# Two dense attentions of 16 heads, one head to 32 rows of the array, units prepared before the attention

## The chip, the core and the metric

The kernel runs on one core of one Trainium2 chip, as one launch. The metric is the device time of that launch in microseconds (us); lower is better. Engines are named as the profile names them: PE is the matrix engine and PEld its weight loads, DVE the vector engine, ACT the scalar engine, POOL GpSimd, SP the queue that issues DMAs.

## The reference, cut to what matters

Twelve sublayers transform x, four batches ("units") of 512 tokens by 128 channels, all in float32. The change is about two of them, the two dense attentions. Both have 16 heads of 8 channels. The first (`mqa`) is causal and shares one key and one value head among all 16; the second (`rope`) is not causal, has its own keys and values for each head, biases, and a rotation of queries and keys.

```python
latent = x @ Wc_down                       # mqa: 128 -> 64
q = (latent @ Wq_up).reshape(B, T, 16, 8); k, v = split(latent @ Wkv_up)
att = softmax(where(causal, einsum('bthd,bsd->bhts', q, k) / sqrt(8), -inf))
x = x + einsum('bhts,bsd->bthd', att, v).reshape(B, T, 128) @ Wc_proj

q, k, v = x @ Wq.T + bq, x @ Wk.T + bk, x @ Wv.T + bv      # rope, 16 heads of 8
att = softmax(einsum('bhsd,bhtd->bhst', rot(q) / sqrt(8), rot(k)))
x = x + einsum('bhst,bhtd->bhsd', att, v).reshape(B, S, 128) @ Wo.T + bo
```

Each input is first normalised over the 128 channels. The other ten sublayers (two mixtures of experts, two channel mixes, two gated MLPs, a forgetting attention, a time mix and two deep six-layer stacks, "deep") are not changed.

## The kernel before

Channels lie on the 128 partitions and tokens along the free dimension, so a unit is a tile of 128 x 512. All sublayers but deep run unit by unit in a hardware loop (`per_unit`), and each unit ends with a wait for its own x, so nothing of unit b + 1 overlaps unit b. Each engine has its own written order of instructions; semaphores tie them together. Every f32 product is issued to PE as two passes (two LDWEIGHTS, two MATMULs), which is why counts of f32 matmuls are twice the number of products.

In the dense attentions (`dense_pe`, `dense_act`, `dense_dve`, lines 410 to 582) a unit goes through these steps, each for all 16 heads:

1. Normalisation (`ln_pe`, `ln_act`, `ln_dve`, lines 141 to 197) and the products for queries, keys and values (lines 414 to 428). For each head DVE writes a copy of the keys in which all other rows are zero (line 556), so that a head's scores are a product over all 128 rows of the array.
2. **Scores for the maxima**: for each of 4 query tiles and 16 heads a product of 128 queries by up to 512 keys (line 444), four heads to four PSUM banks, of which DVE takes the row maxima (line 564). In `mqa` a bf16 product with the identity adds the causal mask to the diagonal block (line 447).
3. The negated maxima are turned by PE (line 452) and copied by ACT into free rows of the queries (line 500), so that the next scores come out with the maximum subtracted.
4. **Keys and values**: for each of 4 key tiles and 16 heads a product keys by queries (line 463, mask line 466), its exponential by ACT (line 506, four buffers), and the product of values with it (line 473), two steps behind. The values lie spread in zeroed columns (lines 511 to 517), so that this too uses the whole array; ones beside them give the denominators.
5. Copy, reciprocal, product (lines 569 to 574), the output projection (line 477) and the addition to x (lines 578, 580).

SP issues all DMAs: x, some 50 constant tensors (line 1297), then layers 0 and 1 of deep (line 1272). PE starts when all constants have landed.

## Time and profile before

| | us |
|---|---|
| median of 3 runs | 6653.96 |
| lowest and highest run | 6646.73, 6661.31 |
| profiled execution, its own time | 6652.98 |
| its span, first to last instruction | 6651.2 |
| of it, `mqa` with its four units | 644.0 (162.0 to 806.0) |
| of it, `rope` with its four units | 830.4 (1011.0 to 1841.4) |
| deep, twice | nearly all after 2300 |
| share of PE, DVE, ACT, POOL busy | 81%, 57%, 35%, 45% |
| granted PE clock, mean | 0.873 of 2.4 GHz |

The profiled execution's own time is 1.8 us more than its span; both are within the three runs. Busy shares are averages over very different stages; the stages have to be read one by one. A granted clock of 1.00 is 2.4 GHz and 0.50 is 1.2 GHz; means between them are mixtures of the two.

### The profile page before, as it was taken

Reading aid. Unit: us, or ns where it says so; the run is one execution under the profiler, and the core shown is the slowest. Engines: PE = TensorE matmul, PEld = TensorE weight load, DVE = VectorE, ACT = ScalarE, POOL = GpSimd, SP = SyncE. Lnnn points to the kernel's source line nnn. Section 1 sums busy time; section 2 is a strip of 40 time slices with the busy share of each in tenths; the row PEclk is TensorE's granted clock in tenths of the full one; section 3 lists DMA queues with packets and bytes.
Section 4 is the critical chain, followed back from the end, with each engine's and each line's share of the span. In section 5 each row is a group of like instructions: output and inputs, shape, how many; then the busy total and the mean of one; then the engine's idle time right before and its main releaser. Section 6 shows DMA issues by size and latency. Waiting matters only on the chain.

```text
span 6651.2 us, 145048 instructions
## 1 busy us (share of the span) xinstructions
PE 5355.9 (81%) x64980; PEld 3035.4 (46%) x64980; DVE 3759.9 (57%) x4061; ACT 2357.0 (35%) x2740; POOL 2981.6 (45%) x1264
## 2 busy tenths in 40 slices
PE   5888868898964678888888888856888888888887
PEld 2455533343432344554555545423455555545454
DVE  4222343321224377777777777645777777777774
ACT  1222221122232344444444444423444444444443
POOL 0000000000000277777777777506777777777773
PEclk8888868999965689999999999967998999999998
DMA  1000000000000011111110111100101111111110
GB/s 64 1 0 0 0 0 0 0 0 0 0 0 0 3 26 26 42 26 42 26 42 23 42 26 26 26 34 13 29 23 42 26 42 26 40 26 42 26 26 23
DMA packets 77764, 142.42 MB, mean 21 GB/s; under 512 B 18632, under 2 KB 25488, under 8 KB 75536
## 3 DMA queue, kind: packets, MB, share of 16 engines
q1 hardware_dynamic: 77200, 133.84, 7.8%
q8 instruction: 483, 7.91, 0.5%
q14 instruction: 81, 0.66, 0.0%
HBM read 38.36 MB, written 1.05 MB: 6 GB/s over the span
## 4 chain that ended last, share of the span: by engine, by line
PE 64%; DVE 16%; ACT 7%; issue 7%; POOL 5%; SPq 0%; DVEq 0%; DMA 0%; POOLq 0%; ACTq 0%
PE psum L828 11%; PE psum L444 6%; PE psum L463 6%; PE psum L473 6%; PE psum L890 5%; PE psum L797 4%; PE psum L878 4%; PE psum L859 4%; DVE arena L1093 3%; ACT arena L983 3%; PE psum L811 3%; PE psum L845 3%; DVE arena L1106 2%; DVE arena L1102 2%; POOL arena L1206 2%
## 5 line engine op out<-in xcount | busy, mean ns | idle before, releaser
L1206 POOL TENSOR_TENSOR arena<-arena,minus_half 128x16 f32<-128x16 f32 x384 | 1125.0, 2930 | 1034.0 <-DVE arena L1095 1031.7
L828 PE MATMUL psum<-deep_wqkv,arena 128*128 128x512 f32 x1536 | 877.8, 701 | 432.2 <-DVE arena L1106 424.2
L1221 POOL MEMSET arena<- 128x33 f32 x4 | 0.4, 128 | 2432.0 <-DVE std L1425 2432.0
L1208 POOL TENSOR_TENSOR arena<-arena 128x1024 f32<-128x1024 f32 x384 | 903.4, 2353 | 0.0
L1211 POOL TENSOR_TENSOR arena<-arena 128x1024 f32<-128x1024 f32 x384 | 889.5, 2316 | 30.1
L983 ACT ACTIVATE arena<-psum 128x1024 f32<-128x1024 f32 x384 | 393.4, 1024 | 1040.1 <-PE psum L828 1040.0
L1093 DVE TENSOR_REDUCE arena<-arena 128x16 f32<-128x1024 f32 x384 | 467.0, 1216 | 448.2 <-ACT arena L983 446.6
L828 PEld LDWEIGHTS psum<-deep_wqkv,arena 128*128 128x128 f32 x1536 | 300.8, 212 | 792.2 <-DVE arena L1106 518.7
L845 PEld LDWEIGHTS psum<-w_ident,arena 128*128 128x128 f32 x3072 | 398.7, 153 | 254.9 <-issue 250.6
L1085 DVE TENSOR_TENSOR arena<-arena 128x1024 f32<-128x1024 f32 x192 | 491.8, 2561 | 6.6
L1102 DVE TENSOR_TENSOR arena<-psum,arena 128x1024 f32<-128x1024 f32 x384 | 467.2, 1217 | 0.0
L1106 DVE TENSOR_TENSOR arena<-psum,arena 128x1024 f32<-128x1024 f32 x384 | 465.8, 1213 | 0.0
L463 PE MATMUL psum<-arena 128*128 128x512 f32 (+3 forms) x1024 | 455.5, 529 | 10.4 <-ACT arena L500 10.4
L569 DVE COPY arena<-psum 64x512 f32<-64x512 f32 x16 | 11.0, 689 | 784.0 <-PE psum L473 783.8
L473 PE MATMUL psum<-arena 128*128 128x512 f32 (+3 forms) x1024 | 453.2, 527 | 0.0
L444 PE MATMUL psum<-arena 128*128 128x512 f32 (+3 forms) x1024 | 409.9, 550 | 40.7 <-DVE arena L556 37.2
L845 PE MATMUL psum<-w_ident,arena 128*128 128x128 f32 x3072 | 433.5, 288 | 2.4 <-ACT arena L1000 2.4
L506 ACT ACTIVATE arena<-psum 128x512 f32<-128x512 f32 (+3 forms) x512 | 264.9, 517 | 477.3 <-PE psum L463 281.6
L1071 DVE TENSOR_REDUCE arena<-psum 128x16 f32<-128x1024 f32 x192 | 235.1, 1225 | 336.5 <-PE psum L797 336.5
L989 ACT ACTIVATE arena<-psum 128x1024 f32<-128x1024 f32 x384 | 392.0, 1021 | 82.5 <-PE psum L845 82.4
L878 PEld LDWEIGHTS psum<-arena 64*64 64x64 f32 x24576 | 380.5, 136 | 61.0 <-issue 60.4
L878 PE MATMUL psum<-arena 64*64 64x32 f32 x24576 | 402.2, 221 | 2.7 <-issue 2.7
(247 smaller groups left out, 8031.5 us busy)
## 6 DMA issues: line engine op xcount, KB each, us to landing
arena<-arena SPq DMA_DIRECT2D x672, 128.0 KB, 2.4
deep_wqkv<-in_deep_wqkv SPq DMA_DIRECT2D x12, 1536.0 KB, 7.0
deep_wo<-in_deep_wo SPq DMA_DIRECT2D x12, 512.0 KB, 7.5
arena<-arena SPq DMA_DIRECT2D x96, 64.0 KB, 2.0
deep_w<-in_deep_w SPq DMA_DIRECT2D x12, 341.0 KB, 7.6
deep_w<-in_deep_w SPq DMA_DIRECT2D x12, 192.0 KB, 7.5
deep_scales<-in_deep_scales SPq DMA_DIRECT2D x12, 128.0 KB, 8.1
x<-in_x SPq DMA_DIRECT2D x4, 256.0 KB, 3.4
```

The source lines that it names most:

```text
L444: last = nc.tensor.matmul(bank(a + j)[:, 0:keys], da_q[:, h // HALF, qt * P:(qt + 1) * P], da_kM[:, h, 0:keys], start=True, stop=not causal)
L463: last = nc.tensor.matmul(a[:, q0:T], da_kM[:, h, kt * P:(kt + 1) * P], da_q[:, h // HALF, q0:T], start=True, stop=not causal)
L473: nc.tensor.matmul(bank(6 + h // HALF)[:, q0:T], da_Vm[:, h, kt, :], da_PT[:, v % BUFS, q0:T], start=(kt == 0 and h % HALF == 0), stop=(kt ...
L828: last = nc.tensor.matmul(bank(2 + cc), xs[unit_ % 2][:, WIN + t * P:WIN + (t + 1) * P], wqkv[:, half * INNER + cc * 512:half * INNER + (c ...
L845: last = nc.tensor.matmul(turns[:, m * P:(m + 1) * P], roped[:, h:h + 2, :], w.ident[:, :], start=True, stop=True, is_transpose=True)
L878: last = nc.tensor.matmul(bank(odd)[64 * side:64 * side + 64, to:to + WIN], V[64 * r:64 * r + 64, WPT * t + jj, (pair + odd) * 64:(pair + ...
L1093: nc.vector.tensor_reduce(h_sum[a % 2][:, hs], qk_sq[:, hs, :], AX.X, ALU.add).then_inc(de.deep_sq_summed, 1)
L1102: nc.vector.tensor_tensor(turned[:, hs, :].rearrange("p h (a e) -> p h a e", a=2), swapped, sin, ALU.mult).then_inc(de.deep_rope_parts, 1)
L1106: nc.vector.tensor_tensor(roped[:, hs, :], qk_half, under(tabs[:, 2 * half, t, :], shape), ALU.mult).then_inc(de.deep_rope_parts, 1)
L1206: nc.gpsimd.tensor_tensor(h_inv[a % 2][:, hs], h_sum[a % 2][:, hs], minus_half[:, :], ALU.pow).then_inc(de.deep_inv_ready, 1)
L1208: nc.gpsimd.tensor_tensor(dst[:, hs, :], dst[:, hs, :], turned[:, hs, :], ALU.add).then_inc(de.deep_summed, 1)
L1211: nc.gpsimd.tensor_tensor(dst[:, hs, :], dst[:, hs, :], over(h_inv[a % 2][:, hs], [P, LHEADS, LD]), ALU.mult).then_inc(de.deep_roped, 1)
```

## The change

Both dense attentions are written anew; the arithmetic stays the same.

**A head gets 32 rows.** Four heads make a set, four sets a unit. Head j of a set has its 8 channels in rows 32j to 32j + 7 of the queries `da_Q` and keys `da_K`, a maximum (queries) or a one (keys) in row 32j + 8, zeros elsewhere. A product then takes 32 rows of the array; four heads can stand in it together. The copies with zeroed rows, the spread values and their memsets are gone. Widening is done by PE (`dense_wide_pe`): in `mqa` by padded weights, in `rope` by products with a 0/1 matrix after the rotation. Values have 32 columns to a head (8 values, a one, zeros); `dense_mix_pe` writes four heads to four groups of 32 output partitions.

**Units are prepared first.** `dense_prepare_*` normalises and projects all four units, the normalisation of unit b + 1 woven into the projections of unit b. Then come all the scores, then for all units the denominators, division and output.

**Stages overlap.** `dense_attend_pe` runs 5 bodies of 4 sets x 4 steps. In a step it issues, in turn, half the scores of one query tile (two heads, two banks) of unit `body`, two keys products of unit `body - 1`, the other half, two more keys products, once per set the turning of the maxima, and the values product of the step before. Scores have 2 pairs of banks, keys 3 banks, values 1. The causal mask follows each half and each keys product, as before a 128-row bf16 product.

**Around it.** The output of a set goes back to `da_Q` (ACT); at the end four products each sum values and spread denominators over the sets (`dense_sum_pe`). Layer 1 of deep now lies in the arena, and SP loads it only once the sublayers before deep are done. Three 128 x 512 f32 constants are new, the value weights and bias of `rope` are four times as wide, two small constants are added and two removed. GpSimd, idle before in these stages, zeroes `mx` once per sublayer.

The diff, cut to its core ("..." marks what is left out):

```diff
-ARENA = 34400
-EARLY = 20700
+ARENA = 39860
+ODD_LAYER = 34430
+EARLY = 30724
...
+        def pair_use(q, x_, h):
+            return (9 * q - 1 if q else 0) + 2 * x_ + h + (1 if q and x_ else 0)
+        def pair_use_max(q):
+            return 9 * (q + 1) - 1 + (2 if q + 1 < NB * SETS else 0)
+        def keys_of(causal, b, s):
+            return da_K[:, b if causal else b * SETS + s, :]
...
+        def dense_prepare_pe(pe, u, n, causal, N):
...
+                        dense_wide_pe(pe, 5 * b + s, w.mqa_q[:, s, :], da_lat[0:64, :], N)
+                    if b + 1 < NB:
+                        ln_pe_var(pe, n + b + 1, 1)
+                    dense_wide_pe(pe, 5 * b + SETS, w.mqa_k[:, :], da_lat[0:64, :], N)
+                    if b + 1 < NB:
+                        ln_pe_spread(pe, n + b + 1, 0)
+                else:
+                    dense_values_pe(pe, b, 0, N)
+                    dense_values_pe(pe, b, 1, N)
+                    dense_rot_pe(pe, b, N)
+                    if b + 1 < NB:
+                        ln_pe_var(pe, n + b + 1, 1)
+                    dense_values_pe(pe, b, 2, N)
+                    dense_values_pe(pe, b, 3, N)
+                    pe.wait_ge(da.rope_step, N.rope_step + 6 * b + 3)
+                    for s in range(SETS):
+                        dense_wide_pe(pe, 8 * b + s, w.ra_widen[:, s, :], da_cos[0], N)
+                    if b + 1 < NB:
+                        ln_pe_spread(pe, n + b + 1, 0)
+                    pe.wait_ge(da.rope_step, N.rope_step + 6 * b + 6)
+                    for s in range(SETS):
+                        dense_wide_pe(pe, 8 * b + SETS + s, w.ra_widen[:, s, :], da_cos[1], N)
...
+        def dense_half_pe(pe, causal, b, s, x_, h, N):
+            v, keys = pair_use(b * SETS + s, x_, h), (x_ + 1) * P if causal else T
+            if v >= 2:
+                pe.wait_ge(da.pairs_free, N.pairs_free + v - 1)
+            apart(pe)
+            kk = keys_of(causal, b, s)
+            for at, j in enumerate(HALF_OF[h]):
+                r32 = slice(32 * j, 32 * j + 32)
+                last = nc.tensor.matmul(bank(2 * (v % 2) + at)[:, 0:keys], da_Q[r32, b * SETS + s, x_ * P:(x_ + 1) * P],
+                                        kk[r32, 0:keys], start=True, stop=not causal)
             if causal:
...
+                for at in range(2):
+                    last = nc.tensor.matmul(bank(2 * (v % 2) + at)[:, x_ * P:keys], identb[:, :], later_key_q[:, :],
+                                            start=False, stop=True)
+            last.then_inc(da.scores_ready, 1)
+        def dense_max_pe(pe, q, N):
+            v = pair_use_max(q)
+            pe.wait_ge(da.pairs_free, N.pairs_free + max(v - 1, pair_use(q, TILES - 1, 1) + 1))
+            for qt in range(TILES):
+                last = nc.tensor.matmul(bank(2 * (v % 2))[:, qt * P:(qt + 1) * P], mx[:, q % SETS * TILES + qt, :], w.ident[:, :],
+                                        start=True, stop=True)
+            last.then_inc(da.max_turned, 1)
+        def dense_keys_pe(pe, causal, b, s, kt, half, N):
+            group = GROUPS * b + TILES * s + kt
+            q0 = kt * P if causal else 0
+            kk = keys_of(causal, b, s)
+            for at in (2 * half, 2 * half + 1):
+                m, j = 4 * group + at, KEY_ORDER[at]
+                if kt == 0 and at == 0:
+                    pe.wait_ge(da.pairs_free, N.pairs_free + pair_use_max(b * SETS + s) + 1)
+                if m >= 3:
+                    pe.wait_ge(da.probs_ready, N.probs_ready + m - 2)
+                apart(pe)
+                r32, to = slice(32 * j, 32 * j + 32), bank(4 + m % 3)
+                last = nc.tensor.matmul(to[:, q0:T], kk[r32, kt * P:(kt + 1) * P], da_Q[r32, b * SETS + s, q0:T],
+                                        start=True, stop=not causal)
+                if causal:
+                    last = nc.tensor.matmul(to[:, q0:q0 + P], identb[:, :], later_key_k[:, :], start=False, stop=True)
+                last.then_inc(da.keys_ready, 1)
+        def dense_mix_pe(pe, causal, group, N):
+            b, s, kt = group // GROUPS, group // TILES % SETS, group % TILES
+            q0 = kt * P if causal else 0
+            pe.wait_ge(da.probs_ready, N.probs_ready + 4 * group + 4)
+            if kt == 0 and group >= TILES:
+                pe.wait_ge(da.y_kept, N.y_kept + group // TILES)
+            apart(pe)
+            for at in range(SETS):
+                j = KEY_ORDER[at]
+                c0 = 0 if causal else s * P + 32 * j
+                last = nc.tensor.matmul(bank(7)[32 * j:32 * j + 32, q0:T], da_V[:, b * TILES + kt, c0:c0 + 32],
+                                        da_PT[:, group % 2 * SETS + at, q0:T], start=(kt == 0), stop=(kt == TILES - 1),
+                                        skip_group_check=True)
+            last.then_inc(da.pv_done, 1)
+        def dense_attend_pe(pe, causal, N):
+            made = 5 * NB if causal else 8 * NB
+            pe.wait_ge(da.wide_kept, N.wide_kept + made)
+            pe.wait_ge(da.v_kept, N.v_kept + (NB if causal else NB * TILES))
+            for body in range(NB + 1):
+                for s in range(SETS):
+                    for x_ in range(TILES):
+                        group = GROUPS * (body - 1) + TILES * s + x_
+                        if body < NB:
+                            dense_half_pe(pe, causal, body, s, x_, 0, N)
+                        if body >= 1:
+                            dense_keys_pe(pe, causal, body - 1, s, x_, 0, N)
+                        if body < NB:
+                            dense_half_pe(pe, causal, body, s, x_, 1, N)
+                        if body >= 1:
+                            dense_keys_pe(pe, causal, body - 1, s, x_, 1, N)
+                        q = body * SETS + s - 1
+                        if x_ == 0 and 0 <= q < NB * SETS:
+                            dense_max_pe(pe, q, N)
+                        if group >= 1:
+                            dense_mix_pe(pe, causal, group - 1, N)
+            dense_mix_pe(pe, causal, GROUPS * NB - 1, N)
...
+        def dense_sum_pe(pe, b, N):
+            pe.wait_ge(da.y_kept, N.y_kept + SETS * (b + 1))
+            if b >= 2:
+                pe.wait_ge(da.y_ready, N.y_ready + b - 1)
+            for to, lhs, done in ((2 * (b % 2), w.da_den, da.den_ready), (2 * (b % 2) + 1, w.da_own, da.ysum_ready)):
+                for s in range(SETS):
+                    last = nc.tensor.matmul(bank(to), lhs[:, s, :], da_Q[:, b * SETS + s, :], start=(s == 0), stop=(s == SETS - 1))
+                last.then_inc(done, 1)
+        def dense_out_pe(pe, u, b, causal, N):
+            pe.wait_ge(da.y_ready, N.y_ready + b + 1)
+            if b >= 2:
+                pe.wait_ge(g.unit_done, u + b - 1)
+            nc.tensor.matmul(bank(4 + b % 2), (w.mqa_proj if causal else w.ra_wo)[:, :], da_y[b % 2], start=True,
+                             stop=True).then_inc(da.out_ready, 1)
...
+        def dense_pe(pe, u, n, causal, N):
+            dense_prepare_pe(pe, u, n, causal, N)
+            dense_attend_pe(pe, causal, N)
+            pe.wait_ge(da.probs_ready, N.probs_ready + 4 * GROUPS * NB)
+            dense_sum_pe(pe, 0, N)
+            for b in range(NB):
+                if b + 1 < NB:
+                    dense_sum_pe(pe, b + 1, N)
+                dense_out_pe(pe, u, b, causal, N)
...
+        def dense_exp_act(act, causal, group, N):
+            q0 = group % TILES * P if causal else 0
+            for at in range(SETS):
+                m = 4 * group + at
+                if at == 0 and group >= 2:
+                    act.wait_ge(da.pv_done, N.pv_done + group - 1)
+                act.wait_ge(da.keys_ready, N.keys_ready + m + 1)
+                nc.scalar.activation(da_PT[:, group % 2 * SETS + at, q0:T], bank(4 + m % 3)[:, q0:T],
+                                     ACT.Exp).then_inc(da.probs_ready, 1)
+        def dense_y_act(act, q, N):
+            act.wait_ge(da.pv_done, N.pv_done + TILES * (q + 1))
+            nc.scalar.activation(da_Q[:, q, :], bank(7), ACT.Copy).then_inc(da.y_kept, 1)
...
+        def dense_max_dve(dve, causal, b, s, x_, h, N):
+            q = b * SETS + s
+            v, keys = pair_use(q, x_, h), (x_ + 1) * P if causal else T
+            dve.wait_ge(da.scores_ready, N.scores_ready + 2 * (TILES * q + x_) + h + 1)
+            if x_ == 0 and h == 0 and q >= SETS:
+                dve.wait_ge(da.max_turned, N.max_turned + q - SETS + 1)
+            first = 32 * HALF_OF[h][0] + HD8
+            nc.vector.tensor_reduce(mx[:, s * TILES + x_, first:first + 33:32], banks(2 * (v % 2), 2)[:, :, 0:keys], AX.X, ALU.max,
+                                    negate=True).then_inc(da.pairs_free, 1)
+        def dense_lay_max_dve(dve, q, N):
+            v = pair_use_max(q)
+            dve.wait_ge(da.max_turned, N.max_turned + q + 1)
+            nc.vector.tensor_tensor(da_Q[:, q, :], bank(2 * (v % 2)), da_Q[:, q, :], ALU.add).then_inc(da.pairs_free, 1)
...
+        def dense_divide_dve(dve, b, N):
+            dve.wait_ge(da.den_ready, N.den_ready + b + 1)
+            nc.vector.reciprocal(da_inv[b % 2], bank(2 * (b % 2))).then_inc(da.inv_ready, 1)
+            dve.wait_ge(da.inv_ready, N.inv_ready + b + 1)
+            dve.wait_ge(da.ysum_ready, N.ysum_ready + b + 1)
+            if b >= 2:
+                dve.wait_ge(da.out_ready, N.out_ready + b - 1)
+            nc.vector.tensor_tensor(da_y[b % 2], bank(2 * (b % 2) + 1), da_inv[b % 2], ALU.mult).then_inc(da.y_ready, 1)
...
                 if c == 0:
                     load_layer(sp, c, 0)
+                    sp.wait_ge(g.unit_done, first_deep)
                     load_layer(sp, c, 1)
...
+    widen, den = np.zeros((P, 4, P), f), np.zeros((P, 4, P), f)
+    for i in p:
+        s, j, e = i // 32, i // 8 % 4, i % 8
+        widen[i, s, 32 * j + e] = 1
+        den[32 * j + 8, s, i] = 1
```

## Rows read from the trace of the kernel before

**Rows 1.** The page: the chain that ended last, shares of the span by engine
```profile
PE 64%; DVE 16%; ACT 7%; issue 7%; POOL 5%; SPq 0%; DVEq 0%; DMA 0%; POOLq 0%; ACTq 0%
```

**Rows 2.** Stages; columns: window, length, then each engine's busy us, PEclk, DMA, GB/s
```profile
162.00:806.00 644.00, 562.77 (x2216) 331.49 (x2216) 171.94 (x192) 140.08 (x296) 0.00 (x0) 0.88 0.00 0
1011.00:1841.40 830.40, 740.45 (x1712) 332.74 (x1712) 244.04 (x224) 182.08 (x292) 0.00 (x0) 0.93 0.00 0
```

**Rows 3.** Groups of instructions by line, shapes apart: name, shapes, busy us, mean ns
```profile
L1071 DVE TENSOR_REDUCE arena<-psum 128x16 f32<-128x1024 f32 x192 | 235.1, 1225 | 336.5 <-PE psum L797 336.5
...
L506 ACT ACTIVATE arena<-psum 128x512 f32<-128x512 f32 x320 | 191.1, 597 | 357.1 <-PE psum L463 281.6 <-PE psum L466 75.5
...
L564 DVE TENSOR_REDUCE arena<-psum 128x4 f32<-128x512 f32 x16 | 10.6, 685 | 9.2 <-PE psum L447 9.2
```

**Rows 4.** The page's costliest groups: the exponentials of both stages together
```profile
L506 ACT ACTIVATE arena<-psum 128x512 f32<-128x512 f32 (+3 forms) x512 | 264.9, 517 | 477.3 <-PE psum L463 281.6
```

**Rows 5.** Chain of waits, 1130 to 1140 us: start, length, what
```profile
1130.33 0.86 PE psum L463 x2
```

**Rows 6.** Timeline from 1138.6 us: start, length, engine, line
```profile
1138.75 1.02 PE L463 MATMUL psum<-arena 128*128 128x512 f32 x2
...
1139.81 0.60 ACT L506 ACTIVATE arena<-psum 128x512 f32<-128x512 f32 x1 [1.12 <-PE psum L463]
```

**Rows 7.** Timeline of PE from 2613.2 us, two of the four tiled steps of deep
```profile
2613.30 2.07 PE L878 MATMUL psum<-arena 64*64 64x32 f32 x128
2615.30 1.94 PE L859 MATMUL psum<-deep_wqkv,arena 128*64 128x512 f32 x8
2617.17 0.61 PE L792 MATMUL psum<-maskb,identb 128*128 128x512 bf16 x2
2617.71 1.48 PE L797 MATMUL psum<-arena 64*32 64x64 f32 x128
2619.12 1.12 PE L895 MATMUL psum<-xn,w_avg 128*128 128x512 f32 x2
```

**Rows 8.** The same view from 2558 us
```profile
2558.12 1.06 PE L792 MATMUL psum<-maskb,identb 128*128 128x512 bf16 x2
2559.11 0.89 PE L797 MATMUL psum<-arena 64*32 64x64 f32 x43
```

**Rows 9.** Stages with few rows or columns; columns as in rows 2
```profile
182.40:187.50 5.10, 5.10 (x12) 3.02 (x12) 0.00 (x0) 1.78 (x3) 0.00 (x0) 0.50 0.00 0
502.40:506.90 4.50, 4.50 (x12) 2.61 (x10) 0.00 (x0) 1.78 (x3) 0.00 (x0) 0.50 0.00 0
143.40:146.80 3.40, 3.05 (x10) 0.93 (x8) 2.99 (x11) 0.23 (x1) 0.00 (x0) 0.50 0.00 0
146.90:150.20 3.30, 2.62 (x7) 1.03 (x7) 1.51 (x1) 0.59 (x1) 0.00 (x0) 1.00 0.00 0
```

**Rows 10.** Timeline of PE from 191.2 us, scores of unit 0 of mqa
```profile
191.41 0.74 PE L444 MATMUL psum<-arena 128*128 128x128 f32 x2
191.94 0.31 PE L447 MATMUL psum<-arena,identb 128*128 128x128 bf16 x1
192.05 0.74 PE L444 MATMUL psum<-arena 128*128 128x128 f32 x2
```

**Rows 11.** Timeline from 1227 us, the seam between two units of rope
```profile
1227.22 2.07 PE L145 MATMUL psum<-x,w_avg 128*128 x2 [0.94 <-DVE x L580]
...
1229.45 0.69 DVE L182 TENSOR_TENSOR xc<-x,psum 128x512 f32<-128x512 f32 x1 [0.74 <-PE psum L145]
...
1230.82 1.28 ACT L174 ACT_TABLE_LOAD   x1
...
1236.13 0.50 PEld L419 LDWEIGHTS psum<-xn,arena 128*128 128x128 f32 x2 [1.07 <-DVE xn L191]
```

**Rows 12.** Timeline from 36 us, the first matmul
```profile
36.08 2.07 PE L145 MATMUL psum<-x,w_avg 128*128 x2 [36.08 <-DVE maskb L1402]
```

**Rows 13.** By line, shapes apart: the reciprocal of the denominators
```profile
L571 DVE RECIPROCAL arena<-arena 128x512 f32<-128x512 f32 x8 | 26.8, 3353 | 0.3
```

406 lines of the change are left out of this document (206 added, 200 removed).

## The prediction

> **What bounds the kernel now.** I read the page, then the stages, then the groups by line, last the timeline. The page's chain [rows 1] lies 64% on PE; but the change touches only `mqa` and `rope`, and what it is worth is read from their 644.0 and 830.4 us [rows 2]. There PE is busy 87% and 89% of the time while DVE has 172 and 244 us of work and ACT 140 and 182: PE bounds them. In the keys phase the chain runs from one f32 product of 512 columns to the next, 0.86 us each [rows 5]; ACT needs 0.60 of every 1.72 us [rows 6]. The seams between units cost more: from the mean to the first projection 8.9 us pass, mostly waits [rows 11].
>
> About 0.2% (13 us) is what a measurement of this kernel can tell from no change. The sum is made against the profiled execution, 6653 us, which is 1 us under the median of the runs.
>
> **Prices.** A product of 512 columns: 0.86 us at 2.4 GHz, in proportion to its columns, twice that at 1.2 GHz. From its start to ACT's start 1.06 us [rows 6]. ACT 0.60 for 512 columns [rows 3]; DVE 0.685 for maxima of 512 elements and 1.225 of 1024 [rows 3], so by the line through both about 0.42 for 256. A PSUM tensor_tensor 0.69, a table load 1.28 [rows 11], a reciprocal 3.35 [rows 13].
>
> **Do products stand side by side?** No row has 32-row products; deep has the nearest. Its 8 passes of 512 columns in two column groups take 1.87 us from their start to the next step's, where one after another they would take 8 x 0.43 = 3.43: 1.8 of 2 at a time. Its 128 passes of 64 columns on eight tiles take 1.41 instead of 128 x 0.054 = 6.9: 4.9 at a time [rows 7]. The bounds are 1 and 4 at a time; I take 4, since wide products lie nearest to the full gain.
>
> **What a change of tiling costs.** Before the two bf16 products of 512 columns (0.43 us of streaming) and after them the array changes from tiles to whole and back: 0.54 us from start to start at 2.4 GHz, 0.99 instead of 0.85 at 1.2 [rows 7, 8], so 0.11 to 0.14 of drain a change. The next f32 weight load (128 columns) cannot hide behind the drain: 0.11 at 2.4, 0.21 at 1.2 GHz. The latter is from scores of 128 columns with a mask, which repeat every 0.64 us, three loads [rows 10]. So a change back to 32-row tiles costs 0.23 (2.4 GHz) or 0.35 (1.2), one to the identity about 0.13 or 0.17. Bounds: 0, if it overlaps, and twice this.
>
> **`rope`.** A middle step: half the scores beside two keys products, the same again, then the values product, 3 x 0.86 = 2.57; two changes of tiling 0.38; and a chain that is new: the fourth keys product needs the bank of the first, so its exponential, 1.06 + 0.60 after the step's start, and starts at 1.7 instead of 0.86. The values product follows at 2.7, the next step at 3.8. DVE has 2.45 + a quarter of 0.69 in it, ACT 2.55: both hidden. Turning the maxima adds 1.0 a set. Set 4 x 3.8 + 1.0 = 16.2; three bodies of four sets 194.
> The first body has scores only, two products at a time with DVE behind: PE streams a quarter of the array's rows twice. At 2.4 GHz DVE would set 12 us a set; at 1.2 GHz the pair of banks comes round in (1.225 + 2.07) / 2 = 1.65, with the maxima 16.2 a set. The last body has keys and values only: 3.8 a step at 2.4 GHz, 6.6 at 1.2 GHz (1.72 + 0.3 + 0.6 to the fourth product, 1.72, 0.15, 1.72, 0.35). I take 1.2 GHz for both (next part): 65 + 106. Preparation: 17 products a unit 14.6, normalisation in small products 1.8, a wait for the standard deviation's table load and copy behind ACT's queue 2.7: 19 x 4, plus 8.9 for the first normalisation and 8 at the low clock: 93. End: 36 products 31, the last division and the low clock at first 6: 37. Sum 93 + 65 + 194 + 106 + 37 = 495, so 335 us less.
>
> **`mqa`, and the clock.** The mask is a product over all 128 rows. It follows each half and, what matters, **each** keys product: the next keys product waits for it, so no two keys products stand side by side, and a step has six changes each way. For a set (widths 128 to 512, one product of each 2.14 us at 2.4 GHz): halves 2 x (4 x 0.46 + 2.14) = 8.0; keys 4 x (4 x 0.40 + 2.14) = 15.0; values 2.7; maxima 1.0: 26.7. That is 107 a body. At 1.2 GHz: halves 2 x (4 x 0.73 + 4.29) = 14.4, keys 4 x (4 x 0.62 + 4.29) = 27.1, values 5.0, maxima 1.9: 48.4 a set.
> Which clock? For 5.1 and 4.5 us PE ran 64-row products without a break at 1.2 GHz, and the clock did not rise; it did rise after a stretch of 128-row products of 8 columns with gaps in it [rows 9]. So what the engine did in full-height products seems to count. In the new `mqa` body most of the time goes to a single 32-row product or to a drain. I take 1.2 GHz: first body 4 x (14.4 + 1.9 + 0.2) = 66, three middle bodies 12 x 48.4 = 581, last 4 x 32.1 = 128: 775. Preparation has 64-row products at 1.2 GHz, about 19 a unit with its waits and 8.9: 85. End 37. Sum 897: **253 us more**. By the Trainium skill ("TensorE: Matmul & The Clock Gate", Part 1) the clock follows how busy the engine is, without a word on rows; rows 9 speak against the plain reading, and by it rival 1 holds.
>
> **The rest.** GpSimd's memset hides under the normalisation. SP issues three more DMAs before PE starts [rows 12] and more bytes: +2. Layer 1 of deep is loaded during deep's first normalisations and needed four units later: nothing, and if that cover fails one load of some 10 us. The copies with zeroed rows, memsets and spread values that go are in the stage sums already.
>
> **Sum:** 6653 + 253 - 335 + 2 = 6573. Against the median it is 81 us less.
>
> **Rivals.**
> 1. *The clock holds.* `mqa` attends in 4 x (10.4 + 80.1 + 17.7) = 433 and takes 540 with 107 around it, 104 less; `rope` with fast ends takes 433, 397 less. Total 6154; between, with `rope` slow at its ends, 6216. For: bf16 masks and the turned maxima are full-height work. Against: [rows 9].
> 2. *Slower: the low clock also in `rope`'s middle bodies.* The place is the 3.8 us step: if the clock doesn't rise in it, it becomes 6.6 and the middle bodies take 12 x (26.4 + 1.9) = 340 instead of 194. Total 6719. It decides from 5.7 us a step (48 x 1.9 = 93 more, so 6666). Against: three of four streams in that step fill four groups.
> 3. *What bounds is no longer PE.* The Trainium skill ("TensorEngine Tiling (Array Packing)", PSUM Bottleneck) says that tiling speeds up TensorE but not the emptying of PSUM, which may then bound. As a mechanism here, from rows: changes of tiling and the bank chain cost nothing, and each body of `rope` takes DVE's 32 x 1.225 + 4 x 0.69 = 42, each of `mqa` ACT's 64 x 0.44 + 4 x 0.60 = 30 [rows 3, 4]. Then `rope` takes 5 x 42 + 130 = 340 and `mqa` 150 + 107: total 5778. Against: the mask's order is in the code.
> 4. *The change doesn't do what it says*: 32-row products don't overlap. `rope`'s step has 12 x 0.86, three bodies 510, `rope` saves nothing, `mqa` pays 290 or more: about 6940. Against [rows 7].
>
> **Chances.** My forecast 0.48, its own range 6470 to 6690 (the changes of tiling are 16 x (8 + 16) x 0.52 = 200 us of `mqa`: half of it is 100 less, half as much again 100 more). Rival 1 with its middle form 0.25, rival 2 0.14, rival 3 0.08, rival 4 0.05. The range 6150 to 6740 takes in the first three. Faster: nine tenths of the forecast, rivals 1 and 3: 0.76; within 0.2%: 0.06; slower 0.18.
>
> **What would show it.** Right: a granted clock near 0.5 in the whole of `mqa`'s attention and near 0.9 in the middle of `rope`'s; in `mqa` keys products never two at a time, in `rope` 3.8 us from one values product to the next; ACT and DVE idle for PE. Wrong: a clock of 1.00 in `mqa` (rival 1), a DVE without idle time (rival 3), equal starts nowhere (rival 4), or deep longer than before.

## The result, and the profile after

The changed kernel takes 6486.7 us (median of 4 runs, 6473.29 to 6496.11) beside 6657.5 for the kernel before on the same chip: 0.9746 of its time, 95% interval 0.9734 to 0.9757, 171 us less. The direction is as forecast and the time lies within the range, but the saving is twice the 81 us of the sum. The profiled execution took 6481.7 us, 91 less than the 6573 predicted.

The windows of the stages, one after another, answer to [rows 2]: us, PE busy, PEld busy, DVE busy, ACT busy, POOL busy, granted clock. The first five are `mqa` (preparation, first body, three middle bodies, last body, end), the next five the same of `rope`, the last two everything behind `rope` and what lies between the two stages.

```profile
164.40:230.50 66.10, 59.05 (x152) 28.27 (x153) 7.38 (x16) 19.64 (x34) 1.80 (x1) 0.63 0.00 0
230.50:292.50 62.00, 60.92 (x223) 26.36 (x223) 27.99 (x35) 1.17 (x1) 0.00 (x0) 0.50 0.00 1
292.50:838.00 545.50, 545.50 (x1620) 205.75 (x1620) 87.79 (x109) 90.55 (x203) 0.00 (x0) 0.50 0.00 0
838.00:961.00 123.00, 123.00 (x337) 43.71 (x336) 0.69 (x1) 30.87 (x69) 0.00 (x0) 0.50 0.00 0
961.00:993.40 32.40, 31.53 (x73) 13.43 (x71) 18.96 (x12) 0.11 (x1) 0.00 (x0) 0.99 0.00 1
1198.30:1278.00 79.70, 73.03 (x200) 33.69 (x200) 31.61 (x52) 30.58 (x49) 1.58 (x1) 0.92 0.00 0
1278.00:1337.00 59.00, 54.27 (x154) 20.97 (x154) 39.54 (x35) 1.28 (x2) 0.00 (x0) 0.57 0.00 0
1337.00:1544.00 207.00, 206.09 (x1241) 69.23 (x1241) 122.52 (x109) 110.87 (x203) 0.00 (x0) 0.99 0.00 1
1544.00:1644.00 100.00, 86.79 (x277) 19.13 (x274) 0.69 (x1) 37.85 (x70) 0.00 (x0) 0.59 0.00 0
1644.00:1676.10 32.10, 31.18 (x72) 13.37 (x70) 19.20 (x12) 1.17 (x1) 0.00 (x0) 0.99 0.00 0
...
1676.10:6479.90 4803.80, 3840.67 (x60476) 2260.82 (x60476) 3176.27 (x3364) 1973.72 (x2071) 2978.56 (x1256) 0.87 0.11 28
993.40:1198.30 204.90, 133.67 (x337) 69.51 (x338) 94.95 (x156) 40.84 (x52) 0.22 (x1) 0.65 0.00 0
```

`mqa` went from 644.0 to 829.0 us, `rope` from 830.4 to 477.8; the rest is what it was within 6 us (4809.8 and 205.0 before), PE starts `mqa` 2.4 us later. 185 - 353 + 2 - 6 = -172. The row to look at is the third: in the middle bodies of `mqa` PE is busy all of 545.5 us and has the low clock, 1.2 GHz, all the time, while DVE and ACT have 88 and 91 us of work. In `rope` the row of the middle bodies shows 0.99.

The page's groups for the keys products and for the exponentials that wait for the mask (after the bar: busy us, mean ns of one, idle before and who ended it):

```profile
L547 PE MATMUL psum<-arena 32*128 32x512 f32 (+3 forms) x1024 | 571.7, 770 | 14.1 <-ACT arena L658 13.2
L658 ACT ACTIVATE arena<-psum 128x512 f32<-128x512 f32 (+3 forms) x512 | 251.0, 517 | 775.8 <-PE psum L550 584.7
```

The waits of ACT in `mqa` from 293 to 960 us (total, times, longest) show that nearly all its waiting, 584.7 of 606.7 us, is for the mask product on line 550, once for each of the 256 exponentials (the longest, 63.1 us, is the time of the first body, in which there are no keys products):

```profile
ACT arena L658 <- PE psum L550: 584.7, 256, 63.1
ACT arena L663 <- PE psum L563: 22.0, 12, 1.8
```

PE's timeline in a middle body of `mqa` (start, us, count of passes) shows how the work stands there. An f32 product is two passes. From one keys product (256 columns) to the next it is 1.36 us; at 1.2 GHz its two passes stream for 0.85 of them (twice the prediction's price at 2.4 GHz), the other 0.51 go to drains, loads and the mask. From a half for the maxima (256 columns, two heads side by side) to the keys product behind its masks it is 1.48 us, 0.63 more than the stream.

```profile
349.76 1.22 PE L517 MATMUL psum<-arena 32*128 32x256 f32 x4
350.92 0.39 PE L521 MATMUL psum<-arena,identb 128*128 128x128 bf16 x2
351.24 1.64 PE L547 MATMUL psum<-arena 32*128 32x384 f32 x2
...
504.95 1.22 PE L547 MATMUL psum<-arena 32*128 32x256 f32 x2
506.10 0.29 PE L550 MATMUL psum<-arena,identb 128*128 128x128 bf16 x1
506.31 1.22 PE L547 MATMUL psum<-arena 32*128 32x256 f32 x2
507.46 0.29 PE L550 MATMUL psum<-arena,identb 128*128 128x128 bf16 x1
507.68 1.51 PE L563 MATMUL psum<-arena 128*32 128x384 f32 x8
```

In `rope` a step looks like this (2.4 GHz); pairs for the maxima (L517) and keys (L547) start 10 ns apart, and the next step starts 4.03 us after this one:

```profile
1376.80 0.70 PE L517 MATMUL psum<-arena 32*128 32x512 f32 x2
1376.81 0.70 PE L547 MATMUL psum<-arena 32*128 32x512 f32 x2
...
1378.81 1.09 PE L547 MATMUL psum<-arena 32*128 32x512 f32 x2
1379.84 1.06 PE L563 MATMUL psum<-arena 128*32 128x512 f32 x8
1380.83 0.70 PE L517 MATMUL psum<-arena 32*128 32x512 f32 x2
```

So the theory to test is the prediction's own: `mqa` is PE's serial time, made long by single masks between the products and by the low clock. Its rivals are that ACT or the banks hold it, and that something else decides the clock. Below, a set is the time from one copy of finished values to the next; windows are laid from copy to copy, and a window of ten sets is named so. For `mqa` after the change ten sets take 455.5 us, for `rope` 172.3:

```profile
349.90:805.40 455.50, 455.50 (x1362) 171.81 (x1364) 73.07 (x91) 75.99 (x171) 0.00 (x0) 0.50 0.00 0
...
1359.70:1532.00 172.30, 171.51 (x1044) 56.54 (x1045) 101.24 (x90) 92.85 (x170) 0.00 (x0) 1.00 0.00 1
```

### The profile page after: what moved, and what is told of

Same layout as the page of the kernel before. It is cut to its first block, busy times and chain, and to the rows that moved or that the text cites. A ratio compares the mean times of both kernels' runs of the same rounds, so it can differ in the third digit from the quotient of the medians.

```text
span 6479.9 us, 145495 instructions
## 1 busy us (share of the span) xinstructions
PE 5332.2 (82%) x65388; PEld 2850.1 (44%) x65388; DVE 3701.0 (57%) x4027; ACT 2357.5 (36%) x2780; POOL 2982.6 (46%) x1265
## 4 chain that ended last, share of the span: by engine, by line
PE 55%; issue 20%; DVE 13%; ACT 6%; POOL 6%; SPq 0%; DMA 0%; DVEq 0%; POOLq 0%
PE psum L1022 11%; PE psum L547 5%; PE psum L1084 5%; PE psum L991 5%; PE psum L1072 4%; PE psum L1053 4%; DVE arena L1287 4%; ACT arena L1177 3%; PE psum L1005 3%; PE psum L517 3%; PE psum L1039 3%; DVE arena L1300 3%; DVE arena L1296 3%; POOL arena L1400 2%; PE psum L986 2%
## 5 line engine op out<-in xcount | busy, mean ns | idle before, releaser
L1177 ACT ACTIVATE arena<-psum 128x1024 f32<-128x1024 f32 x384 | 393.5, 1025 | 1040.8 <-PE psum L1022 1040.7
L1022 PE MATMUL psum<-deep_wqkv,arena 128*128 128x512 f32 x768 | 453.5, 721 | 248.5 <-DVE arena L1300 240.6
L547 PE MATMUL psum<-arena 32*128 32x512 f32 (+3 forms) x1024 | 571.7, 770 | 14.1 <-ACT arena L658 13.2
L1022 PE MATMUL psum<-arena 128*128 128x512 f32 x768 | 424.5, 680 | 184.0 <-DVE arena L1300 184.0
L729 DVE TENSOR_REDUCE arena<-psum 128x2 f32<-128x1024 f32 (+3 forms) x256 | 257.1, 1024 | 523.1 <-PE psum L521 424.7
L658 ACT ACTIVATE arena<-psum 128x512 f32<-128x512 f32 (+3 forms) x512 | 251.0, 517 | 775.8 <-PE psum L550 584.7
L1183 ACT ACTIVATE arena<-psum 128x1024 f32<-128x1024 f32 x384 | 391.6, 1020 | 81.1 <-PE psum L1039 81.1
L1194 ACT ACTIVATE arena<-psum 128x1024 f32<-128x1024 f32 x192 | 196.6, 1024 | 451.6 <-PE psum L1005 451.6
```

The lines of the kernel that those rows point to most:

```text
L547: last = nc.tensor.matmul(to[:, q0:T], kk[r32, kt * P:(kt + 1) * P], da_Q[r32, b * SETS + s, q0:T], start=True, stop=not causal)
L1022: last = nc.tensor.matmul(bank(2 + cc), xs[unit_ % 2][:, WIN + t * P:WIN + (t + 1) * P], wqkv[:, half * INNER + cc * 512:half * INNER + (c ...
L1177: nc.scalar.activation(qk_sq[:, HALVES[half], :], qk_half, ACT.Square).then_inc(de.deep_qk_squared, 1)
```

## The experiments

Unless another kernel is named, each diff is against the changed kernel, and times of a single run are given as such. H stands for the two products of a half for the maxima, K for the two of a half of the keys, M for one mask.

### Masks in pairs

```diff
+            masks = []
             for at in (2 * half, 2 * half + 1):
...
                 if causal:
-                    last = nc.tensor.matmul(to[:, q0:q0 + P], identb[:, :], later_key_k[:, :], start=False, stop=True)
-                last.then_inc(da.keys_ready, 1)
+                    masks.append(to[:, q0:q0 + P])
+                else:
+                    last.then_inc(da.keys_ready, 1)
+            for to_mask in masks:
+                nc.tensor.matmul(to_mask, identb[:, :], later_key_k[:, :], start=False, stop=True).then_inc(da.keys_ready, 1)
```

> The edit changes the order on TensorE alone: the two keys products of a half first, then their two masks, instead of product, mask, product, mask. Nothing is left out. Theory A (the masks' changes of tiling hold the mqa stage): a half loses two of its three changes (each 0.11 to 0.14 us and an exposed load of 0.14 to 0.16, 128 halves) and its two keys products of 32 rows run side by side, which saves one product's mean stream of 0.53 us at 1.2 GHz in 128 halves (68 us). The attention of mqa goes from 730 us to about 630 (range 600 to 660), the kernel to about 6385 us, rope unchanged at 478. Rival B (products on two groups of 32 rows do not run side by side in this kernel): only the changes go, 730 to about 695, kernel 6450. Rival C (ACT's exponentials or the banks of keys hold mqa, not TensorE): no change within 5 us. The granted clock of mqa's middle bodies stays 0.50 by A and B.

Measured: 6170.2 us (median of 4, 6148.9 to 6217.2), 0.9282 of the kernel before, interval 0.9231 to 0.9332. The attention of `mqa` took 427 us, after 730 in the changed kernel; theory A had 600 to 660. The windows, first three sets (344.0 to 445.3 us), then seven (464.4 to 597.8):

```profile
344.00:445.30 101.30, 101.30 (x410) 38.20 (x412) 21.77 (x28) 20.14 (x51) 0.00 (x0) 0.50 0.00 1
464.40:597.80 133.40, 133.40 (x942) 57.78 (x944) 50.31 (x62) 47.03 (x120) 0.00 (x0) 1.00 0.00 1
```

33.8 us a set at the low clock instead of 45.6, and 19.1 at the high one. At the low clock a half of keys thus lost (45.6 - 33.8) / 8 = 1.47 us. The expectation had a slip of two in it: 0.53 us is one of the two passes of the mean keys product; the whole stream is 1.07, which leaves 0.40 for the two changes of tiling, 0.20 each with the exposed load. The timeline agrees: 0.51 around a single masked product, less 0.11 of the mask's own stream. That a change of tiling drains the engine is what the Trainium skill states ("TensorEngine Tiling (Array Packing)", Key Properties), without a size; here drain and exposed load together took 0.20 us. The other miss is the clock: it rose, between 440 and 450 us, 140 us into the middle bodies. With the order alone the attention would be, by estimate, 62 + 12 x 33.8 + 4 x 21 = 552 us (21 for a set of the last body at the low clock, from the run with products first, below), so of the 303 us that it lost some 180 are the order's and some 120 the clock's. Rival C is out: nothing but PE's order changed. Rival B is out with it, since 1.47 us is more than the 0.40 of the two changes.

### No masks on the keys, no masks at all

```diff
...
-                if causal:
-                    last = nc.tensor.matmul(to[:, q0:q0 + P], identb[:, :], later_key_k[:, :], start=False, stop=True)
                 last.then_inc(da.keys_ready, 1)
```

> This kernel leaves the 256 masks of mqa's keys products out (the masks of the halves, which only serve the maxima, stay), so its attention is not causal. Theory A: a half of keys then is one stream of 0.53 us for both products and about 0.25 us around it at 1.2 GHz, instead of 2.1 us, which takes 128 x 1.3 = 166 us off: attention of mqa 730 to about 565 us if the granted clock stays at 0.50. Rival D: with full-height products gone from the keys the array is fed by four 32-row groups as in rope, and the granted clock rises to 1.0 in the three middle bodies: attention 330 to 400 us. Rival C (ACT holds it): over 700 us.

The second kernel takes out L521 of the halves in the same way.

> This kernel leaves all masks of mqa out, those of the halves and those of the keys products, so its attention is not causal. Theory A: beside the 166 us of the run before, 64 x 2 halves lose two masks of 0.11 us and two changes of tiling (about 0.6 us together at 1.2 GHz, 128 times, 77 us, of which some 17 lie in the first body, where VectorE sets the pace): attention about 490 us at clock 0.50. Rival D: the granted clock of the middle bodies is 1.0 as in rope; then with 5/8 of rope's columns the three middle bodies take 45 to 65 us each, and the attention 290 to 350 us.

One run each: 6259.9 and 6043.7 us. Ten sets of the first, then of the second:

```profile
329.80:632.90 303.10, 303.10 (x1202) 122.47 (x1202) 73.02 (x91) 67.22 (x170) 0.00 (x0) 0.50 0.00 1
```

```profile
311.60:446.90 135.30, 129.29 (x1044) 62.73 (x1047) 69.78 (x91) 68.08 (x170) 0.00 (x0) 1.00 0.00 1
```

30.3 us a set and the low clock throughout (attention 502 us, where theory A had 565, again for the slip of two), against 13.5 at the high clock (attention 287: rival D, 3 us under its range). So leaving the keys' masks out is *slower* than keeping them in pairs (6260 beside 6170), since with the pairs the clock rose and here it did not.

### The mask as a product on GpSimd

No masks on PE; for each group, behind its four exponentials:

```diff
...
+                    pool.wait_ge(da.probs_ready, N.probs_ready + 4 * group + 4)
+                    nc.gpsimd.tensor_tensor(da_PT[:, a0:a0 + SETS, q0:q0 + P], da_PT[:, a0:a0 + SETS, q0:q0 + P],
+                                            under(later_key_k[:, :], [P, SETS, P]), ALU.mult).then_inc(da.masked, 1)
...
-    c["later_key_k"] = np.where(p[:, None] > p[None, :], -FAR, 0).astype(f)
+    c["later_key_k"] = np.where(p[:, None] > p[None, :], 0, 1).astype(f)
```

The values product waits for `masked`.

> All mask products of mqa go from TensorE; instead GpSimd, idle in this stage, multiplies the four 128 x 128 diagonal blocks of a group of exponentials with zeros and ones, one instruction for a group (64 in all), and the values product waits for it. Nothing is left out: a maximum over unmasked keys of the same block serves as well. Theory A: as the run without any masks, plus little, since a group's values product comes one group later anyway: attention 290 to 350 us if the clock rises (kernel about 6080), about 490 if it doesn't (kernel 6245). Rival E: a 128 x 512 multiply on GpSimd takes over 3 us and each group waits for it: middle bodies at 16 x 3 or more, and the attention 50 us or more longer than in the run without masks. Rival F: GpSimd's reads of SBUF slow VectorE's maxima in the first body.

Measured: 6051.1 us (median of 4), 0.9093 of before (0.9078 to 0.9108), attention of `mqa` 292 us. Ten sets take 137.0, clock 0.99. GpSimd's group, and the one wait of PE for it:

```profile
L778 POOL TENSOR_TENSOR arena<-arena 128x512 f32<-128x512 f32 x64 | 69.8, 1090 | 297.0 <-ACT arena L655 297.0
```

```profile
PE psum L560 <- POOL arena L778: 0.6, 1, 0.6
```

1.09 us each, 64 times, behind other work: rival E is out. So is rival F: in the first body GpSimd has no mask to do, and in ten sets of the middle bodies VectorE is busy 69.8 us with the multiplications as without them. Clearing PE of the masks gives all that leaving them out gave, within 5 us in the attention.

### Maxima and values one after the other

`maxima(i)` issues the two halves of group i and, once per set, the turning; `values(i)` its four keys products and the values product of the group before.

```diff
...
+            maxima(0)
+            for body in range(NB):
+                for i in range(GROUPS * body + 1, GROUPS * (body + 1) + 1):
+                    maxima(i)
+                for i in range(GROUPS * body, GROUPS * (body + 1)):
+                    values(i)
```

> The changed kernel with one edit: TensorE's order. The maxima of a body (and of the first group of the next) come first, then its keys and values, so that the two no longer run beside each other; the same instructions, nothing left out. Theory A (mqa's attention is TensorE's serial time at 1.2 GHz, so running side by side brings it nothing): the first body of mqa shows 15.5 us a set for maxima alone and the last 30.2 a set for keys and values alone, together 45.7, against 45.6 in the middle bodies. So mqa's attention stays at 730 us (within 15). In rope the first body shows 14.8 a set and the last 27.0, together 41.8 against 17.2 in the middle: attention 16 x 41.8 = 668 us instead of 366, if the clock stays low, 500 to 600 if it rises for parts of it. Kernel about 6790 (6620 to 6800). Rival G (the side by side running serves mqa too, TensorE waits there): mqa grows by over 50 us.

One run: 6769.3 us. The attention of `mqa` took 737 us instead of 730: the side by side bodies bring `mqa` nothing, as theory A has it, and rival G is out. `rope`'s took 629 instead of 366. Keys and values alone in `rope`, two sets at the low clock and one set mostly at the high one:

```profile
1386.10:1440.10 54.00, 47.39 (x131) 9.69 (x131) 0.00 (x0) 18.57 (x34) 0.00 (x0) 0.50 0.00 0
...
1580.50:1598.00 17.50, 14.19 (x67) 3.26 (x67) 0.00 (x0) 9.29 (x17) 0.00 (x0) 0.90 0.00 1
```

27.0 and 17.5 us a set. `rope` with 263 us more would still be 90 us under the kernel before: of its saving about three quarters hang on the side by side bodies, their clock included.

### Products first, then the masks

H and K of a half return their masks instead of issuing them; then

```diff
-                        if body < NB:
-                            dense_half_pe(pe, causal, body, s, x_, 0, N)
-                        if body >= 1:
-                            dense_keys_pe(pe, causal, body - 1, s, x_, 0, N)
...
+                        for h in range(2):
+                            masks = []
+                            if body < NB:
+                                masks += dense_half_pe(pe, causal, body, s, x_, h, N)
+                            if body >= 1:
+                                masks += dense_keys_pe(pe, causal, body - 1, s, x_, h, N)
+                            dense_masks_pe(masks)
```

> The changed kernel with one edit in TensorE's order, in mqa alone: the two products of a half for the maxima and the two of a half for the keys, which lie on other groups of rows, come first, then all their four masks. Nothing is left out. The masks in pairs gave 33.8 us a set at the low clock (45.6 before it) and 19.1 once the clock had risen, 200 us into the attention. Theory A' (changes of tiling and lack of overlap both cost time and keep the clock low): two more changes and one stream of 0.53 us go from each half, 8 halves a set: about 27 us a set at the low clock, 15 at the high one. Theory H (denser side by side products raise the clock): it rises within the first of the middle bodies, as without masks; then 12 x 15 and some 125 for first and last bodies: attention about 305 us (290 to 340), kernel about 6050 (6030 to 6090). Rival I: masks of full height as such keep the clock down for the first 200 us again: 350 to 450 us, kernel 6095 to 6195.

Measured: 6102.0 us (median of 4), 0.9164 of before (0.9149 to 0.9179). Attention of `mqa` 336 us, within theory H's range but at its upper end, since the last body stayed at the low clock at 21 us a set; ten sets:

```profile
329.40:488.00 158.60, 158.60 (x1364) 70.37 (x1368) 73.00 (x91) 67.16 (x170) 0.00 (x0) 1.00 0.01 1
```

15.9 us a set with every product and every mask of the changed kernel, 385 us less for an order on one engine. The clock was at 0.98 from 320 us on, 20 us after the first keys product. There halves for the maxima and for the keys start 20 ns apart, and their masks follow in fours:

```profile
320.00:340.00 20.00, 20.00 (x176) 8.57 (x168) 9.31 (x12) 7.68 (x22) 0.00 (x0) 0.98 0.00 1
...
400.29 0.70 PE L517 MATMUL psum<-arena 32*128 32x512 f32 x2
400.31 0.49 PE L547 MATMUL psum<-arena 32*128 32x128 f32 x4
...
401.35 0.40 PE L557 MATMUL psum<-arena,identb 128*128 128x128 bf16 x4
```

The kernel's time misses theory H's range by 12 us and lies in that of rival I; what rules rival I out is the clock, which rose after 20 us and not after 200, and the attention, 14 us under its range.

### The order of heads, and the order alone

The kernel without the keys' masks (30.3 us a set, clock 0.50), twice more with the same instructions. First:

```diff
-        KEY_ORDER = (2, 3, 0, 1)
+        KEY_ORDER = (0, 1, 2, 3)
```

> The run without the masks of the keys (30.3 us a set in mqa, clock 0.50 throughout, 6260 us), with the heads of the keys in the order 0, 1, 2, 3 instead of 2, 3, 0, 1; it leaves out the same part. The instructions and the number of changes of tiling are the same; only now a half of keys (heads 0 and 1) is followed by a half for the maxima on other rows (heads 2 and 3), where before it was followed by one on the same rows and had to end first. Theory H (side by side products raise the clock): a set costs about 26 us at the low clock (8 x 0.53 less), and the clock rises to 1.0 in the middle bodies, where a set takes 14 to 16 us: attention of mqa 300 to 350 instead of 502, kernel 6060 to 6110. Rival J (the number of changes of tiling decides the clock, not the overlap): clock 0.50, set 26, attention 450, kernel 6205. Rival K (no overlap): unchanged, 6260. In rope, where the order of rows makes the same overlaps one half later, 17.2 us a set either way.

One run: 6290.0 us, and no theory was right: the clock is rival J's, the set and the kernel's time are nobody's. Ten sets of `mqa`, then of `rope`:

```profile
334.50:620.90 286.40, 286.40 (x1202) 106.54 (x1204) 73.04 (x91) 68.44 (x171) 0.00 (x0) 0.50 0.00 1
1126.00:1330.30 204.30, 171.82 (x1044) 57.65 (x1047) 101.23 (x90) 92.85 (x171) 0.00 (x0) 1.00 0.00 1
```

Once in a step a half of keys now ran into the next H; passes of both start 10 ns apart:

```profile
429.46 0.80 PE L547 MATMUL psum<-arena 32*128 32x256 f32 x2
429.47 1.01 PE L517 MATMUL psum<-arena 32*128 32x384 f32 x2
```

But a set still took 28.6 us, and the clock stayed low (attention 482 us after 502). In `rope`, where I had expected no change, a set took 20.4 instead of 17.2, with PE idle for 32 of the 204 us; in a stretch of 100 us there it waited 14.6 us for exponentials, which it does not do after the change. Its attention took 412 us where the kernel with the other order of heads has 365, so the loss is `rope`'s. Theory H as worded fell: some side by side running is not enough. The next run goes back to the first order of heads and moves the masks behind K, H K M M in place of H M M K, with the edit of the section before; the keys' masks are left out again:

> The run without the masks of mqa's keys (30.3 us a set, granted clock 0.50 throughout, 6260 us) again, and the same part left out; the one edit is the order of its two middle pieces in mqa: the half for the maxima, the half of the keys, then the two masks of the former, where before the masks stood between the two halves. The same instructions. With another order of the heads (6290 us, 28.6 us a set) a half of keys could run into the next half for the maxima, and the clock stayed at 0.50. Theory H' (four products that start together, half for maxima beside half for keys, let the clock rise, whatever stands around them): the clock rises within the first middle body, as in the run with products first and masks after (15.9 us a set); a set takes 14.5 to 15.5 us, the kernel 6070 to 6095. Rival J' (it was the greater number of full-height masks that let the clock rise there and in the run with pairs, and this kernel has half of them): the clock stays at 0.50, a set takes about 23 us, the kernel about 6185.

One run: 6070.8 us, and the ten sets:

```profile
322.30:467.10 144.80, 144.80 (x1204) 61.18 (x1208) 73.05 (x91) 69.40 (x171) 0.00 (x0) 1.00 0.01 1
```

14.5 us a set, clock 1.00. The same 1202 to 1204 passes took 303 or 145 us by their order and the clock that came with it. Rival J' is out: there are as many masks as in the run with the low clock. Rival J is out as well, since both orders change the tiling twice in a half.

### Masks of zeros in `rope`

```diff
...
+                else:
+                    last = nc.tensor.matmul(to[:, 0:P], identb[:, :], later_key_k[:, P - 1:P].broadcast_to([P, P]),
+                                            start=False, stop=True)
```

> The changed kernel, with the mask's kind of work put into rope, where there is none: after each keys product a full-height bf16 product of 128 columns, of zeros, accumulates on it, as in mqa. Nothing is left out. Theory A: no two keys products stand side by side any more and each has two changes of tiling. At the low clock a set of rope takes 16 keys products of 1.71 + 0.51 = 35.5, 8 halves of about 2.0 = 16, values 7.5 and the turned maxima 1.9: 61 us instead of 17.2, and the granted clock of the middle bodies is 0.50: kernel 6487 + 12 x 44 + 4 x 16 = about 7080 (6950 to 7150). Rival M (the clock stays high, since rope's streams are longer): a set takes about 30 us, kernel 6690.

One run: 6752.8 us, under theory A's range and above rival M. The clock was neither: it changed to and fro. Two sets, then one:

```profile
1399.60:1452.00 52.40, 52.40 (x243) 17.03 (x246) 21.00 (x18) 20.32 (x34) 0.00 (x0) 0.93 0.00 1
...
1480.30:1522.40 42.10, 42.10 (x123) 11.60 (x123) 10.50 (x9) 10.15 (x17) 0.00 (x0) 0.54 0.00 1
```

26.2 us a set at 0.93 and 42.1 at 0.54, in place of 17.2. My 61 for the low clock was too much: it let H and K of other rows never overlap, and the records show that they do (at 1489.15 and 1489.16 us H and the first keys product start together, at the low clock). With the zero products in pairs:

> As the run before, but with the zero products of rope (and the masks of mqa's keys) in pairs behind the two keys products of a half. Theory A: a half of keys is 1.71 + 0.6 = 2.3 us at the low clock, a set 44 us, and 22 to 24 at the high one. In mqa the pairs let the clock rise late, so I expect the high clock in most of rope's middle bodies: about 12 x 7 us more than the 6170 of the masks in pairs, and 20 more in the last body: about 6275, and up to 6560 if the clock stays low throughout. Rival N (a full-height product per item costs rope as much in pairs as singly): as the run before less the mqa part, over 6700.

The kernel that ran differs from this text in one thing: its masks in `mqa` were still single, so it is to be compared with 6487, not with 6170. One run: 6526.8 us, 40 more, 14 of them in `rope`'s middle bodies and 18 in its last. Ten sets of `rope`:

```profile
1365.80:1550.40 184.60, 184.60 (x1204) 61.09 (x1206) 105.01 (x90) 92.74 (x170) 0.00 (x0) 1.00 0.00 1
```

18.5 us a set instead of 17.2, under the 22 to 24 expected, where single ones cost 9 to 25 more. So single masks slow `rope` as they slow `mqa`, and paired ones hardly do. Rival N is out.

### Products whose results nobody reads

To the kernel with the mask on GpSimd, in the last bodies:

```diff
...
+                        if body == NB and not (s == 0 and x_ == 0):
...
+                            for j in range(SETS):
+                                r32, kk = slice(32 * j, 32 * j + 32), keys_of(causal, NB - 1, 0)
+                                nc.tensor.matmul(bank(j)[:, 0:T // 2], kk[r32, 0:P], kk[r32, 0:T // 2], start=True, stop=True)
```

> The kernel whose masks are multiplied on GpSimd, with work added: in the last body of mqa and of rope, where the granted clock is 0.50 to 0.65 and a set takes 18.7 and 27 us at the low clock, each step but the first also issues four products of 32 rows and 256 columns, side by side, into the banks of the maxima, whose results nobody reads. Nothing is left out. Theory H (the low clock of the last bodies is from too little side by side work): the clock rises, a set takes 11 to 14 in mqa and 15 to 18 in rope: the last bodies go from 72 and 88 to 45 to 57 and 62 to 72 us, the kernel from 6051 to about 6015 (6000 to 6030). Rival L: the added products only add their time, 15 x 0.45 us at 1.2 GHz in each stage: 6065.

Then four such products in each step of the first bodies as well, in banks 4 to 7:

> The kernel with multiplied masks and products added in the last bodies (6005 us), with four more added in each step of the first bodies of mqa and of rope (32 rows, 256 columns, side by side, into banks that nobody uses then). Nothing is left out. The first bodies take 47 and 60 us at a granted clock of 0.50 to 0.57, while VectorE, busy 27 and 39 us in them, waits for TensorE for 15 and 22 us. Theory H (side by side work raises the clock): the clock rises within the first 20 us, VectorE's waits shrink by half: 40 and 50 us, kernel about 5988. Rival L: the clock stays, and each step pays 0.85 us more: 16 x 0.85 = 14 us in each stage, kernel 6032.

Measured: 6005.2 us (median of 4), 0.9039 of before (0.9006 to 0.9073), and 5988.4 (median of 5), 0.9013 (0.8992 to 0.9034). Two sets of `mqa`'s last body without the added products, and two with them:

```profile
482.30:519.60 37.30, 32.42 (x130) 10.08 (x130) 0.00 (x0) 13.43 (x34) 8.72 (x8) 0.50 0.00 0
```

```profile
473.20:499.50 26.30, 21.02 (x195) 9.02 (x195) 0.00 (x0) 13.45 (x34) 8.69 (x9) 1.00 0.01 1
```

Half as many passes more (195 for 130) in 11 us less. `rope`'s last body went from 27.0 us a set at 0.50 to 17.7 at 1.00. The first bodies, `mqa` and `rope`, of the second kernel:

```profile
230.70:266.90 36.20, 32.97 (x282) 20.43 (x283) 26.46 (x35) 1.15 (x1) 0.00 (x0) 0.95 0.00 1
802.80:847.20 44.40, 43.28 (x282) 20.87 (x285) 38.96 (x35) 1.19 (x1) 0.00 (x0) 1.00 0.00 1
```

47 and 60 us became 36 and 44. Rival L is out for both (its price for the last bodies, 0.45 us, should have been 0.85 at 1.2 GHz, which puts it further off). The intervals of the two kernels overlap, so in whole-kernel time the second step is not told from the first; the windows of the profiled execution, the fastest of its five, do tell it. 5988 us is the shortest time of this study, about 500 under the changed kernel.

## Why the prediction was right and wrong

**Which stage gains and which loses** was right. `rope` was to save 335 us and saved 353, `mqa` to lose 253 and lost 185. The attention of `rope` came out at 366 us against 65 + 194 + 106 = 365, but by luck, since its parts offset each other: first 59, middle 207, last 100. The middle step is 4.03 us, not 3.8: the fourth keys product starts 2.01 us after the step, where its bank's exponential was to let it go at 1.7. That exponential starts at 1378.07 us, 1.26 us after the step's first keys product and not 1.06, and ends 0.14 us before the fourth starts.

**The step that failed** is the term for `mqa`: 897 us against 829. By parts: preparation 85 against 66, first body 66 against 62, the middle 581 against 545, last 128 against 123, end 37 against 32. The largest piece is the middle one: 48.4 us a set against 45.6. In it "keys 4 x (4 x 0.62 + 4.29)" had too dear a change of tiling. The timeline shows 0.51 in place of 0.62 for a keys product, and for a half 0.63 in place of 0.73; 16 x 0.11 + 8 x 0.10 = 2.6 of the 2.8 us. I had taken the load of a short masked product in the kernel before [rows 10] for every change; masks in pairs put a change, load included, at 0.20 us on average where I had 0.17 and 0.35 for its two directions. The mechanism, the masks' place and the clock of 0.50 all held.

**The rivals** fell on the signs named for them: `mqa`'s clock was 0.50 (rival 1), that of `rope`'s middle bodies 0.99 (rival 2), VectorE was busy 88 of 545.5 us in `mqa`'s middle and 123 of 207 in `rope`'s (rival 3), and products on other rows started 10 ns apart (rival 4). Two products of the working are slightly off, neither in the forecast: 48 x 1.9 is 91, not 93, and 64 x 0.44 + 4 x 0.60 is 30.6.

**The other terms** were, as stage sums, all too high too: preparation 19 and 13 us too dear, the ends 5 each. For `mqa`'s preparation I took the low clock throughout, and the window shows 0.63. For `rope`'s I took the high clock with 8 us for a low start, the window shows 0.92, and where its 13 us lie stays open. In executions of other kernels `mqa`'s preparation, the same instructions, took 76 to 78 us at 0.52 to 0.55, so part of the 19 us changes from one execution to the next. The rest of the kernel was 6 us shorter, for which I have no cause. 68 + 17 + 6 = 91 us: between the stages no term hid another's error, they were all on one side; within `rope`'s attention they did.

**The clock** of each stage was as forecast, 0.50 through `mqa`'s attention, 0.99 in the middle of `rope` and 0.57 to 0.59 at its ends. My reason, that full-height products count, was not: with all full-height masks out the clock was highest, and with all masks behind products in fours it was high too. The stretch before the rise in [rows 9] was also read too narrowly: it begins inside full-height products of 512 columns that run until 144.8 us. The Trainium skill ("TensorE: Matmul & The Clock Gate", Part 1) has the clock follow how busy the engine is. Busy by the records it was, 545.5 of 545.5 us at 0.50, so for this kernel the rule in its plain reading does not hold; the measurement decides.

What the runs show of it, in `mqa`'s middle bodies unless said otherwise:

| order within a half | us a set | granted clock |
|---|---|---|
| H M M, K M, K M (single masks) | 45.6 | 0.50 throughout |
| H M M, K K | 30.3 | 0.50 throughout |
| the same, K running into the next H | 28.6 | 0.50 throughout |
| H M M, K K M M | 33.8, then 19.1 | rises after 140 us |
| H and K together, M M | 14.5 | 1.00 within 30 us |
| H and K together, M M M M | 15.9 | 1.00 within 20 us |
| H and K together, no mask | 13.5 | 1.00 |
| `rope`: K M, K M with zeros | 26.2 and 42.1 | changes to and fro |

In `mqa`, wherever four 32-row products start together, half after half, the clock rose within 30 us; wherever a single one or a pair stands alone between drains, it stayed low or rose late. This is what the orders have in common, not a rule that is shown: the orders with four together also put the most streaming into a microsecond, and no run here tells the two apart. The number of changes of tiling is not what decides: the second and the fifth line both have two in a half. Four together once a step (the added products) were enough in the first and last bodies of the kernels without masks on PE, and not enough in the third line. Why the fourth line rises at all, and the third not, is open. The fourth line's runs spread over 68 us where those of the changed kernel spread over 23; the slowest of its four has the lowest mean granted clock, 0.842, and the two fastest the highest, 0.852, which fits a rise at another moment in each.

**Not tried:** the preparation of all units ahead by itself, the changed load of deep's layer 1, and the new code in one of the two attentions with the old code in the other.

## What to carry to other kernels

A short full-height product between packed small ones costs little in streaming and much in what it takes apart (here 0.11 us of stream for one mask, and 1.47 us for a half whose two masks stand single): put all packed products of a stretch first, masks after them, or give the mask to an idle engine. Count what the order does before what the operations cost; here an order on one engine, with the clock that it brought, was worth 385 us. Where a packed stage shows a granted clock of 0.50 with PE fully busy, look for products that could start together, before anything is removed.

## What the hardware showed unexpectedly

- PE can be busy without a gap in the records for 545 us and keep 1.2 GHz. With the keys' masks left out, one order of the same passes ran at 1.2 GHz and another at 2.4 (303 against 145 us for ten sets).
- Adding products made a stretch faster: 37.3 to 26.3 us for two sets with half as many passes more.
- Removing work gained less than reordering it: 6260 us without the keys' masks (one run), 6170 with them in pairs.
- A change between 32-row tiles and the whole array cost 0.20 us at 1.2 GHz with the weight load that it exposes (masks in pairs against single ones).
